# Decoder layer on one core: the weighted sums of two chunks in one visit to the column tiles

## The reference, cut to what matters

```
# x: (8, 512, 256), context: (8, 1601, 256), H = 16 heads of d = 16
q = x @ Wq.T + bq
k = context @ Wk.T + bk
v = context @ Wv.T + bv
scores = einsum('bhtd,bhcd->bhtc', q, k) / sqrt(d)
attn = softmax(scores, axis=-1)
out = einsum('bhtc,bhcd->bhtd', attn, v)
return out.reshape(B, T, D) @ Wo.T + bo
```

## Time and profile before

| | us |
|---|---|
| median of 3 runs | 2213.64 |
| lowest and highest run | 2205.82, 2221.99 |
| the profiled execution's own time | 2199.31 |
| its span | 2197.5 |
| busy in the span: TensorE | 2041.6 (93%) |
| busy: VectorE | 1523.5 (69%) |
| busy: ScalarE | 1226.0 (56%) |
| busy: GpSimd | 439.9 (20%) |

### The profile page before, as it was taken

How to read it: one execution, slowest core, us unless ns; L and a number is a source line. 1 busy time by engine, 2 the same in 40 slices (tenths; PEclk the granted TensorE clock), 3 DMA queues, 4 the chain that set the end, 5 groups by cost and what they waited for, 6 DMA issues and landing times. The chain is left out here.

```text
span 2197.5 us, 36726 instructions
## 1 busy us (share of the span) xinstructions
PE 2041.6 (93%) x12946; PEld 1114.6 (51%) x12946; DVE 1523.5 (69%) x2930; ACT 1226.0 (56%) x2353; POOL 439.9 (20%) x484
## 2 busy tenths in 40 slices
PE   6898895899999999999999999999999879799999
PEld 4665664434444444444444434444433258588887
DVE  6888884677777787787787787787789266522222
ACT  2311312167767777777777777777777733222222
POOL 1100102203103112113113113112110044222222
PEclk9999997589989999999999999999999979899999
DMA  5000003434322522522521621621620010000000
GB/s 174 1 0 0 0 1 80 81 73 94 77 61 76 94 61 71 99 61 70 101 61 64 106 61 58 113 61 57 114 31 2 1 63 17 1 10 19 10 19 19
DMA packets 45373, 118.69 MB, mean 54 GB/s; under 512 B 9120, under 2 KB 21408, under 8 KB 45088
## 3 DMA queue, kind: packets, MB, share of 16 engines
q1 hardware_dynamic: 45232, 116.88, 23.7%
HBM read 77.30 MB, written 38.81 MB: 53 GB/s over the span
## 5 line engine op out<-in xcount | busy, mean ns | idle before, releaser
L1155 DVE TENSOR_REDUCE x_mx<-x_ps 128x1 f32<-128x512 f32 x1536 | 976.1, 685 | 217.2 <-PE x_ps L900 208.1
L1060 ACT ACTIVATE x_probs<-x_ps 128x512 f32<-128x512 f32 (+1 forms) x1664 | 894.3, 597 | 280.6 <-PE x_ps L964 274.6
L964 PE MATMUL x_ps<-x_qst,x_kst 50*128 50x512 f32 (+1 forms) x1664 | 595.6, 453 | 24.2 <-ACT x_probs L1060 22.1
L900 PE MATMUL x_ps<-x_kst,x_qst 48*128 48x512 f32 x1536 | 574.6, 462 | 16.8 <-DMA x_kst<-k_parts 11.1
L900 PEld LDWEIGHTS x_ps<-x_kst,x_qst 48*128 48x128 f32 x1536 | 240.3, 191 | 434.1 <-DVE x_mx L1155 289.2
L948 PE MATMUL x_ps<-x_probs,x_vst 128*17 128x512 f32 (+1 forms) x3328 | 446.2, 608 | 4.8 <-ACT x_ou L1043 4.8
L964 PEld LDWEIGHTS x_ps<-x_qst,x_kst 50*128 50x128 f32 (+1 forms) x1664 | 243.0, 183 | 116.4 <-ACT x_probs L1060 111.0
L1582 DVE TENSOR_TENSOR f_hid_whole<-f_ps,f_act_g 128x512 f32<-128x512 f32 x80 | 55.1, 690 | 240.8 <-PE f_ps L1339 232.2
L1454 ACT ACTIVATE f_act_g<-f_ps 128x512 f32<-128x512 f32 x80 | 47.6, 596 | 243.9 <-PE f_ps L1370 232.0
L1520 POOL TENSOR_TENSOR f_hid_rest<-f_hid_whole,f_hid_rounded 128x512 fp32r<-128x512 f32 x80 | 103.1, 1289 | 233.2 <-ACT f_hid_rounded L1460 233.2
L1092 POOL TENSOR_TENSOR x_vst<-x_v_all,x_bv 128x768 f32<-128x768 f32 x64 | 66.5, 1068 | 379.1 <-ACT x_v_all L1018 300.4
(11 more groups left out here) (191 smaller groups left out, 2487.1 us busy)
## 6 DMA issues: line engine op xcount, KB each, us to landing
x_kst<-k_parts SPq DMA_DIRECT2D x192, 200.1 KB, 8.4
k_parts<-x_kp SPq DMA_DIRECT2D x16, 1601.0 KB, 6.0
x_ctxT<-in_ctxT SPq DMA_DIRECT2D x8, 1601.0 KB, 8.6
x_qst<-q_parts SPq DMA_DIRECT2D x192, 64.0 KB, 2.6
q_parts<-x_qp SPq DMA_DIRECT2D x8, 1024.0 KB, 4.3
x_all<-in_x SPq DMA_DIRECT2D x8, 512.0 KB, 3.9
out<-x_all SPq DMA_DIRECT2D x8, 512.0 KB, 2.9
x_qst<-x_mrows SPq DMA_DIRECT2D x128, 4.0 KB
```

The lines of the kernel that those rows point to most:

```text
L900: m = pe.matmul(o, qst[mg][rows, pair, t * P:(t + 1) * P], kst[mg][rows, pair, i * 512:(i + 1) * 512], start=True, stop=True)
L964: pe.matmul(ps[0:w, n % S_BANKS, :], kst[g][rows, pair, c * P:c * P + w], qst[g][rows, pair, :], start=True, stop=True).then_inc(s_filled, 1)
L1060: nc.scalar.activation(probs[0:w, s % (2 * GH), :], ps[0:w, s % S_BANKS, :], ACT.Exp, scale=HD ** -0.5).then_inc(exp_done, 1)
L1155: nc.vector.tensor_reduce(out=mx[:, 2 * pair + half, t, i:i + 1], in_=o, axis=AX.X, op=ALU.max).then_inc(drained_v, 1)
```

## The change

The visits of two chunks are put together. At the end of each even chunk c of a group, from 2 on, the sums of chunks c - 2 and c - 1 are computed, one behind the other; an odd chunk ends without a visit. The visit for the last chunk of a group stays alone at the end of chunk 0 of the next group. A group then goes 7 times to the column tiles instead of 13. The exponentials have to live longer, so `x_probs` gets 12 slots instead of 8 (three chunks), and ScalarE waits for the visit of three chunks before instead of two. The buffers of `x_rest` become 2 instead of 4. No instruction is added or removed, and `pieces_of` isn't touched.

```diff
-WHOLE = 4
+WHOLE = 2
+SLOTS = 3 * GH
...
-        probs = sb("x_probs", [P, 2 * GH, T])
+        probs = sb("x_probs", [P, SLOTS, T])
...
-                    slot = (GH * x + issued(j)) % (2 * GH)
+                    slot = (GH * x + issued(j)) % SLOTS
...
                         n = woven(b, g, c, 1, n + len(pieces), second)
-                        if c:
+                        if c and c % 2 == 0:
+                            values(b, g, c - 2)
                             values(b, g, c - 1)
-                        elif b or g:
+                        elif c == 0 and (b or g):
                             values(b - (g == 0), (g - 1) % G, SC - 1)
...
-                                if x >= 2:
-                                    act.wait_ge(pv_used, x - 1)
-                                nc.scalar.activation(probs[0:w, s % (2 * GH), :], ps[0:w, s % S_BANKS, :],
+                                if s >= SLOTS:
+                                    act.wait_ge(pv_used, x - SLOTS // GH + 1)
+                                nc.scalar.activation(probs[0:w, s % SLOTS, :], ps[0:w, s % S_BANKS, :],
```

## The result

The changed kernel takes 2296.36 us (median of 4 runs, 2290.98 to 2299.22) against 2216.71 us (4 runs) of the kernel before: ratio 1.0363, 95% interval 1.0317 to 1.0409. It is **slower by 80 us**; I had forecast 43.5 us slower. The time lies in the range, near its upper end. The profiled execution takes 2295.63 us, its span 2293.8 us, 96.3 us more than before; its mean granted clock is 0.946 against 0.963. The profiled execution of the kernel before (2199.31 us) was quicker than each of its 47 executions beside the experiments, whose clocks go from 0.947 to 0.964, median 0.956. So the two profiles lie further apart (96.3 us) than the two medians (80 us).

The account below looks back on a forecast made before the run. TensorE's list was taken to bound the cross attention (busy 395.6 of 400 us). Joins 14.7 + 33.6, less 4.8 for the copy wait, gave +43.5 us: profiled 2199.3 to 2242.8, median 2257 us, range 2232 to 2300.

Parts of the forecast that it names:

- The run of two blocks: Two neighbouring blocks of score matmuls on TensorE: 1.65 us, the fourth score waiting for the first exponential to free a bank.
- the second visit: Second half of a double visit on TensorE: taken as 0.88 us, bounds 0.76 to 1.08.
- an ordinary join: Two blocks made neighbours by a removed visit, not into chunk 2: +0.21 us each with the second visit, 160 of them, 33.6 us.
- the free join: Rival at the fourth score of neighbouring blocks: no wait for the bank, 2153 us in all; chance 0.05.
- the even case: Rival: no change within 1%, second visit 0.76 us or less or exponentials starting sooner, 2234 down to 2214 us; chance 0.11.
- the clock case: Rival: close waits in chunk pairs without pieces lower TensorE's clock, up to +57 us, taken as 2300 us; chance 0.17.
- The joins' term: 192 places where blocks become neighbours, second visit included: 32 into chunk 2 at +0.46 us (14.7), 160 elsewhere at +0.21 (33.6).
- one price serves for all: Claim that joins outside chunk 2 cost +0.21 us each, with or without pieces in the chunks (+0.21 to +0.22).
- The clock's term: Loss from TensorE's lower clock in pairs without pieces: only a rival, +57 us or half, taken as 2300 us; chance 0.17.
- my own sign: Stated test: the forecast is wrong if the clock in the cross attention falls below the old one.
- VectorE stays below: Claim that VectorE doesn't bound the cross attention: sixteen maxima take 10.36 us, eight of two chunks 5.2.

Follow-up runs that it names:

- visits_twice: Kernel before with each of its 416 visits made twice in a row on the same data: 2547.75 us, ratio 1.1525.
- joins_only: Changed kernel with the first visit of each pair left out, so only the joins of blocks remain: 2142.58 us, ratio 0.9692.
- buffers_only: Kernel before with only the change's buffers (12 exponential slots, 2 projection buffers), all visits in their old places: 2207.0 us against 2209.74, ratio 0.999.
- half_exp_before: Kernel before with exponentials of only 256 of the 512 queries: 2177.03 us, ratio 0.983.
- half_visits_no_piece: Kernel before with the visit cut into two by query columns in all chunks from 2 on without a piece: 2188.02 us, ratio 0.9896.

## Why the prediction was right or wrong

**Right: the mechanism and its sizes at equal clock.** The run of two blocks is 1.65 us, the second visit 0.86 (I took 0.88), an ordinary join +0.19 (+0.21). Exponentials cut to half shorten the run, and the two prices by themselves (visits_twice, joins_only) come out as the trace has them, in the pairs at the higher clock. The rivals of the free join and of the even case fall. The buffers cost nothing, as said. That the measured time lies in the range is partly the range's doing: the forecast by itself went up to 2295, the range to 2300 so as to hold half of the clock case, and 2296 came of that case and of joins that I had too cheap.

**The joins' term was too small.** I wrote that "one price serves for all" joins but those into chunk 2. Behind a short piece and into chunk 10 a join costs 0.4 us, not 0.21 (the earlier trace rows showed a long piece only): 42 such joins (21 into chunk 10, 21 in group 0), and 10 more into chunk 10 behind a chunk without a piece, mostly at 0.61. That is 42 x 0.2 + 10 x 0.4 = 12 us. Into chunk 2 it is 0.54 instead of 0.46 at 14 places and 0.44 at 7, 1 us more. The ordinary ones are some 0.02 us cheaper, 2 us less. Together some 54 us at equal clock instead of 43.5.

**The clock's term was missing from the sum.** It stood as a rival with a chance of 0.17, and it is the larger part of the miss; by my own sign (the clock in the cross attention below the old one) the forecast of 2257 us is wrong there. In the two profiles the stretch grew by 90 us: 54 for the waits and, for 73 us more at the lower level, 36 at half a microsecond each. By the medians the clock went from 0.956 to 0.946, some 54 us more at the lower level over the whole span, so up to 27 us; with 54 that is 81, against 80 measured. The price of half is an upper bound that fits here (the double visit of 3.04 us against 1.84; buffers_only with 4 us for 10); in joins_only it was about a third. That the clock and the pairs without pieces belong together is shown: 104 us with 60 such pairs alone, 46 with the 132 others, and in the changed kernel no time at the lower level outside pairs that have a chunk without a piece. That it is several waits in close succession, rather than something else in these places, is argued from the timelines; shorter waits lowered it from 100 to 31 us. I had seen that a stretch with one wait per chunk keeps the clock and let that speak against the rival, though the changed kernel has up to five waits in a row in the same place.

**A wrong reading, and an engine left out.** I read 10.36 us for sixteen maxima as VectorE's pace, 0.65 each. The view merges instructions with small gaps between them; VectorE was keeping TensorE's pace. At 0.61 each four need 2.44 us, and the bank wait, not VectorE, set the 2.63 us of a chunk without a piece. The forecast of the pairs there didn't hang on it, but my expectations for half_exp_before and half_visits_no_piece did. The step from it, "VectorE stays below", compares eight maxima with two whole chunks. It fails at chunk 10, where six maxima in a row keep VectorE for 3.68 us and the sixth matmul must wait for the third reduction; the sum has no term for that.

## What to carry to other kernels

Work between two groups of matmuls that share few banks is worth as much as the wait that it hides; before putting two such pieces of work together to save an edge (0.11 to 0.13 us here), look at how long the group behind would be held without them (0.42 us here), in a place of the same trace where they already follow each other, and do it for every engine that frees a bank and for every length of the work in between. Look then the other way too: cutting the filler in two where nothing else separates the groups was faster by 1.0%, in part by a higher clock. And where several waits come close together, count the clock as part of the sum: it cost about half as much as the waits themselves (up to 27 us against 54).

## What the runs showed of the hardware

The granted clock depends on where the waits are more than on how many there are. 132 joins in stretches with pieces left TensorE at the lower level for 46 us, 60 in stretches without pieces for 104 us; the kernel before had 27 us, and 37 in another trace of the same order. Doubling all visits, which makes TensorE busier, left it at 0.973 over the span, higher than the 0.963 of the kernel before, with 3 us at the lower level in the stretch. An edge between row tiles and column tiles costs little: a half visit of 256 columns takes 0.56 us where a whole one takes 0.98, so, if the rest goes with the columns, 0.14 us of either is the edge. On the edge the Trainium skill, page "TensorEngine Tiling (Array Packing)", section "Key Properties", says that a change of mode drains TensorE; these runs agree that it costs something, and give this as its size. VectorE takes maxima of 128 x 512 from PSUM at 0.61 us each in a row, ScalarE exponentials at 0.49.
